# Edge stage of a graph transformer block: VectorE weighs and adds its four slots in 16 small instructions

## The reference, cut to what matters

```python
e = jnp.einsum('ehd,ehd->eh', k[src], q[dst]) / jnp.sqrt(jnp.float32(H * D))
emax = jax.ops.segment_max(e, dst, num_segments=N)
ex = jnp.exp(e - emax[dst])
denom = jax.ops.segment_sum(ex, dst, num_segments=N)
a = ex / denom[dst]
m = v[src] * a[..., None]
ft2 = jax.ops.segment_sum(m, dst, num_segments=N).reshape(N, F)
```

## Time and profile before

| | us |
|---|---|
| median of 3 runs | 2310.03 (2309.44 to 2310.37) |
| profiled execution | 2306.91 |
| its span, first to last instruction | 2305.0 |
| VectorE busy | 1798.8 (78%) |
| TensorE busy (matmuls) | 1829.8 (79%) |
| ScalarE busy | 1505.6 (65%) |
| GpSimd busy | 1304.2 (57%) |
| edge stage, first gather to last fold | about 105 to 1461 |

### The profile page before, as it was taken

The page is one execution under the profiler, slowest core; times in us unless marked ns, Lnnn a source line. Parts: engine busy times, 40 slices in busy tenths (PEclk is TensorE's granted clock), DMA queues, the critical chain, the costliest instruction groups (busy, mean ns, idle before and its releaser), DMA issues. The chain is left out here.

```text
span 2305.0 us, 43942 instructions
## 1 busy us (share of the span) xinstructions
PE 1829.8 (79%) x12285; PEld 1288.0 (56%) x12285; DVE 1798.8 (78%) x3579; ACT 1505.6 (65%) x5102; POOL 1304.2 (57%) x1281
## 2 busy tenths in 40 slices
PE   7768787788776688887888871387999769999996
PEld 3423333333333566666666650233888669999995
DVE  7389999999998999999999998555899864444442
ACT  2267787777776587787877874587555355555553
POOL 0177777777777777777777777276000014444442
PEclk9878898999988688897978975599999889999998
DMA  8677777777777777777777777475010282222223
GB/s 231 189 229 226 225 229 230 226 222 228 219 225 225 211 226 224 231 226 231 228 230 235 222 234 220 123 201 161 12 32 29 69 294 42 37 36 36 36 37 77
DMA packets 213270, 394.32 MB, mean 171 GB/s; under 512 B 46354, under 2 KB 140637, under 8 KB 213005
## 3 DMA queue, kind: packets, MB, share of 16 engines
q0 software_dynamic: 91392, 278.99, 43.0%
q1 hardware_dynamic: 96848, 90.41, 13.3%
q10 hardware_dynamic: 24829, 22.64, 3.0%
HBM read 346.47 MB, written 48.65 MB: 171 GB/s over the span
## 5 line engine op out<-in xcount | busy, mean ns | idle before, releaser
L802 POOL DMA_INDIRECT ring<-kv_tab,idx x1008 | 1029.3, 1021 | 412.4 <-issue 294.6
L1120 ACT ACTIVATE val<-ring,val 128x64 f32<-128x64 f32 x2016 | 530.1, 337 | 55.6 <-DVE part L901 51.9
L853 DVE TENSOR_TENSOR prod<-ring,tile_bank 128x1024 f32<-128x1024 f32 x252 | 302.1, 1215 | 32.8 <-DMA ring<-kv_tab,idx 32.2
L860 DVE TENSOR_REDUCE score<-prod 128x16 f32<-128x1024 f32 x252 | 299.1, 1211 | 0.0
L2137 POOL DMA_INDIRECT x_sum<-e_yw,to_row x56 | 123.7, 2210 | 219.3 <-DVE e_yw L2163 197.9
L2122 POOL DMA_INDIRECT xr<-rows,from_row x56 | 57.3, 1024 | 286.7 <-issue 286.4
L2212 PE MATMUL e_h<-e_xT,e_now 128*128 128x128 f32 x1792 | 210.9, 277 | 0.8 <-DVE e_now L2153 0.8
L2212 PEld LDWEIGHTS e_h<-e_xT,e_now 128*128 128x128 f32 x1792 | 206.1, 193 | 1.2 <-DVE e_now L2153 1.2
L2227 PE MATMUL e_yps<-e_now,e_hT 128*128 128x256 f32 x896 | 202.5, 379 | 0.0
L890 DVE TENSOR_TENSOR val<-val 128x1040 f32<-128x1040 f32 x126 | 155.9, 1237 | 52.6 <-ACT val L1120 52.4
L2177 ACT ACTIVATE e_now<-e_w_all 128x2048 f32 x56 | 106.9, 1912 | 131.2 <-PE e_yps L2227 131.2
(11 more groups left out here) (423 smaller groups left out, 4719.1 us busy)
## 6 DMA issues: line engine op xcount, KB each, us to landing
loaded<-parts SPq DMA_DIRECT2D x150, 130.0 KB, 2.3
e_w_all<-L_ffn_W SPq DMA_DIRECT2D x16, 1024.0 KB, 12.2
parts<-part ACTq DMA_DIRECT2D x126, 130.0 KB
q_win<-q_tab SPq DMA_DIRECT2D x126, 128.0 KB
ring<-kv_tab,idx POOLq DMA_INDIRECT x1008
kv_tab<-kv_t SPq DMA_DIRECT2D x25, 224.0 KB
xn_buf<-x SPq DMA_DIRECT2D x25, 125.0 KB
x_sum<-x_buf SPq DMA_DIRECT2D x25, 125.0 KB
```

The lines of the kernel that those rows point to most:

```text
L802: pool.indirect_dma_start(out=ring[:, n % RING, e, :], out_offset=None, in_=t.kv_tab, in_offset=bass.IndirectOffsetOnAxis(ap=idx[n % 6][:, ...
L853: dve.tensor_tensor(prod[half][:, :, :], ring[:, n % RING, at, 0:F], bcast(q_ps[n % 2].unsqueeze(1), 128, L // 2, F), ALU.mult).then_inc(q ...
L860: dve.tensor_reduce(score[:, at, :], prod[half][:, :, :].rearrange("p s (h d) -> p s h d", h=HG), AX.X, ALU.add).then_inc(reduced, 1)
L1120: one = act.activation(val[n % 2][:, e, h, 0:DG], ring[:, n % RING, e, F + h * DG:F + (h + 1) * DG], ACT.Copy, scale=val[n % 2][:, e, h, D ...
```

## The change

`weigh` and `fold` go. In their place `weigh_onto` computes, for one slot and head of VectorE's half at a time, value times factor plus ScalarE's weighed value of the slot four further on, 64 elements with the factor read as one number for each partition from column `DG` of `val`. There are 16 such instructions in a tile, eight (slots 0 and 1) in the place of `weigh`, eight (slots 2 and 3) in the place of `fold`. Since their factor column must stay until they are done, `add_factors` first sums the 16 factor pairs into `part_w`, and `keep_factors` copies them back behind the 16. Each run of eight waits for ScalarE's slots that it adds; ScalarE now signals after every slot. The exponentials into `w_ps`, its PSUM region and its semaphore go, and with them the waits of `times_q`, `exps` and `q_of_rows` on them. GpSimd's wait counts the new signals.

```diff
--- before.py
+++ after.py
@@ -717,6 +717,7 @@
         foreign = [s.sb(f"foreign{i}", [128, L]) for i in range(6)]
         prod = [s.sb(f"prod{i}", [128, L // 2, F]) for i in range(2)]
         score = s.sb("score", [128, L, HG])
+        part_w = s.sb("part_w", [128, L // 2, HG])
         own = s.sb("own", [128, L, HG])
         less = [s.sb(f"less{i}", [128, L, HG]) for i in range(2)]
         val = [s.sb(f"val{i}", [128, L, HG, DG + 1]) for i in range(2)]
@@ -754,7 +755,6 @@
         q_ps = [b[:, 0:F] for b in tile_banks]
         where_ps, local_ps = ([tile_banks[(n + 1 - AHEAD) % 2][:, at:at + size] for n in range(2)]
                               for at, size in ((F, 2 * L + 1), (F + 64, 128)))
-        w_ps = [tile_banks[(n + 1) % 2][:, F + 192:F + 192 + L // 2 * HG].rearrange("p (s h) -> p s h", h=HG) for n in range(2)]
         kf_ps = bank_f[0:TP, 0:NPAIR]
         gT_ps = [b[:, 0:NPAIR] for b in (bank_g, bank_o)]
         normT_ps = bank_f2[:, 0:NPAIR]
@@ -772,8 +772,8 @@
 
         blocks_in, q_in, landed, part_out = (x.blocks_in, s.sems("q_win_in", 3), s.gather_sems("landed", 8),
                                              s.sems("part_out", 3))
-        compared, found, idx_ready, spread_ready, find_read, placed, gap_ready, places, w_ready = (
-            s.sem("e_" + n) for n in ("compared", "found", "idx", "spread", "find_read", "placed", "gap", "places", "w_ps"))
+        compared, found, idx_ready, spread_ready, find_read, placed, gap_ready, places, factors_added = (
+            s.sem("e_" + n) for n in ("compared", "found", "idx", "spread", "find_read", "placed", "gap", "places", "factors"))
         q_ready, q_read, reduced, scored, top_ready, less_ready, exp_ready, val_ready, act_val_ready, folded, folding, sum_ready, part_ready, carrier = (
             s.sem("e_" + n) for n in ("q", "q_read", "reduced", "scored", "top", "less", "exp", "val", "act_val", "folded", "folding", "sum", "part", "carrier"))
         level_split, level_in = s.sem("level_split"), s.sem("level_in")
@@ -795,8 +795,8 @@
         def _(pool):
             for n in range(TILES):
                 pool.wait_ge(idx_ready, n + 1)
-                wait(pool, val_ready, n - RING + 1)
-                wait(pool, act_val_ready, n - RING + 1)
+                wait(pool, val_ready, 2 * (n - RING + 1))
+                wait(pool, act_val_ready, 4 * (n - RING + 1))
                 pool.sem_inc(carrier, 1)
                 for e in range(L):
                     pool.indirect_dma_start(out=ring[:, n % RING, e, :], out_offset=None, in_=t.kv_tab,
@@ -848,7 +848,6 @@
                 dve.wait_ge(landed[n % RING * 2 + half], 16 * (L // 2) * (n // RING + 1))
                 dve.wait_ge(q_ready, n + 1)
                 dve.wait_ge(find_read, min(n + AHEAD, TILES))
-                wait(dve, w_ready, n)
                 wait(dve, reduced, 2 * n + half - 1)
                 dve.tensor_tensor(prod[half][:, :, :], ring[:, n % RING, at, 0:F], bcast(q_ps[n % 2].unsqueeze(1), 128, L // 2, F),
                                   ALU.mult).then_inc(q_read, 1)
@@ -877,20 +876,29 @@
                 dve.tensor_tensor(less[n % 2][:, :, :], own[:, :, :], bcast(t.m_all[:, n, :].unsqueeze(1), 128, L, HG),
                                   ALU.subtract).then_inc(less_ready, 1)
 
-            def weigh(n):
-                dve.wait_ge(w_ready, n + 1)
-                dve.tensor_tensor(val[n % 2][:, 0:L // 2, :, 0:DG],
-                                  ring[:, n % RING, 0:L // 2, F:2 * F].rearrange("p s (h d) -> p s h d", h=HG),
-                                  bcast(w_ps[n % 2].unsqueeze(3), 128, L // 2, HG, DG), ALU.mult).then_inc(val_ready, 1)
-
-            def fold(n):
-                v = val[n % 2][:, :, :, :].rearrange("p s h d -> p s (h d)")
-                dve.wait_ge(val_ready, n + 1)
-                dve.wait_ge(act_val_ready, n + 1)
-                dve.tensor_tensor(v[:, 0:4, :], v[:, 0:4, :], v[:, 4:8, :], ALU.add).then_inc(folding, 1)
+            def add_factors(n):
+                v = val[n % 2]
+                dve.wait_ge(exp_ready, n + 1)
+                dve.tensor_tensor(part_w[:, :, :], v[:, 0:4, :, DG], v[:, 4:8, :, DG], ALU.add).then_inc(factors_added, 1)
+
+            def weigh_onto(n, slots):
+                v = val[n % 2]
+                dve.wait_ge(exp_ready, n + 1)
+                dve.wait_ge(act_val_ready, 4 * n + slots.stop)
+                for e in slots:
+                    for h in range(HG):
+                        one = dve.scalar_tensor_tensor(v[:, e, h, 0:DG], ring[:, n % RING, e, F + h * DG:F + (h + 1) * DG], v[:, e, h, DG:DG + 1],
+                                                       v[:, L // 2 + e, h, 0:DG], ALU.mult, ALU.add)
+                one.then_inc(val_ready, 1)
+
+            def keep_factors(n):
+                dve.wait_ge(val_ready, 2 * n + 2)
+                dve.wait_ge(factors_added, n + 1)
+                dve.tensor_copy(val[n % 2][:, 0:4, :, DG], part_w[:, :, :]).then_inc(folding, 1)
 
             def fold_on(n):
                 v = val[n % 2][:, :, :, :].rearrange("p s h d -> p s (h d)")
+                dve.wait_ge(val_ready, 2 * n + 2)
                 dve.wait_ge(folding, 2 * n + 1)
                 dve.tensor_tensor(v[:, 0:2, :], v[:, 0:2, :], v[:, 2:4, :], ALU.add).then_inc(folding, 1)
 
@@ -1071,7 +1079,8 @@
                 if now:
                     keep_own(n)
                 if old:
-                    weigh(n - 1)
+                    add_factors(n - 1)
+                    weigh_onto(n - 1, range(0, 2))
                 if now:
                     top(n)
                 mix(n, 2, 1)
@@ -1080,7 +1089,8 @@
                 mix(n, 2, 2)
                 mix(n, 3, 0)
                 if old:
-                    fold(n - 1)
+                    weigh_onto(n - 1, range(2, 4))
+                    keep_factors(n - 1)
                 if n + AHEAD + 1 < TILES:
                     compare(n + AHEAD + 1)
                 if old:
@@ -1107,8 +1117,6 @@
 
             def exps(n):
                 act.wait_ge(less_ready, n + 1)
-                act.wait_ge(q_ready, min(n + 2, TILES))
-                act.activation(w_ps[n % 2], less[n % 2][:, 0:L // 2, :], ACT.Exp, scale=1.0 / float(F) ** 0.5).then_inc(w_ready, 1)
                 wait(act, folded, n - 1)
                 act.activation(val[n % 2][:, :, :, DG], less[n % 2][:, :, :], ACT.Exp, scale=1.0 / float(F) ** 0.5).then_inc(exp_ready, 1)
 
@@ -1119,8 +1127,7 @@
                 for h in range(HG):
                     one = act.activation(val[n % 2][:, e, h, 0:DG], ring[:, n % RING, e, F + h * DG:F + (h + 1) * DG], ACT.Copy,
                                          scale=val[n % 2][:, e, h, DG:DG + 1])
-                if e == L - 1:
-                    one.then_inc(act_val_ready, 1)
+                one.then_inc(act_val_ready, 1)
 
             def keep_part(n):
                 act.wait_ge(folded, n + 1)
@@ -1213,7 +1220,6 @@
                 pe.wait_ge(q_in[n % 3], 16 * (n // 3 + 1))
                 pe.wait_ge(spread_ready, n + 1)
                 wait(pe, q_read, 2 * n - 2)
-                wait(pe, val_ready, n - 2)
                 pe.matmul(q_ps[n % 2], spread[n % 6][:, :], q_win[n % 3][:, :], start=True, stop=True).then_inc(q_ready, 1)
 
             def late(u, kind):
```

## The result

| | before | after |
|---|---|---|
| median, us | 2309.74 (2305.88 to 2310.37) | 2396.32 (2394.77 to 2402.74) |
| ratio | | 1.0372 (1.0355 to 1.0389) |
| profiled execution, us | 2306.91 | 2402.74 |
| span, us | 2305.0 | 2400.9 |

The forecast was 2408, with a range of 2350 to 2470. The profiled execution is the slowest of the four, 6.4 us above their median.

The account below looks back on a forecast made before the run. VectorE and GpSimd were taken to bound the edge stage together. Its four stretches, +50, +3, +44 and +1, sum to +98 us on the profiled 2306.91, giving 2405; the run median lies 3.1 above, 2408, range 2350 to 2470.

Parts of the forecast that it names:

- What bounds the stage: Edge stage: GpSimd at 10.6 us a tile and VectorE at 10.15 and 9.70 are at their limit together.
- The step of the 16: Added VectorE instructions of 64 elements: 0.195 us each start to start, 3.12 us a tile, ends 2.3 and 4.5.
- Sums, copy and the wait: VectorE: factor sum and copy 0.09 us each, wait for the last of the 16 0.085; together 0.27 a tile.
- Collisions: VectorE's small instructions meeting gathers: some 2.5 a tile at 0.04 to 0.07, 0.1 us, ends 0 and 0.3.
- VectorE net: VectorE's added work less the removed weighing and fold: +1.21 us a tile, ends 0.2 and 2.9.
- GpSimd near 10.6, VectorE ahead: Gathers: a hit costs about 0.2 us, two or three a tile; GpSimd stays near 10.6, VectorE at 11.4 sets the pace.
- Slack: VectorE's idle time in the edge stage's four stretches absorbs part of the added work, leaving +50, +3, +44 and +1 us.
- Held gathers: Rival, edge stage: runs of eight hold GpSimd out, which then needs 11.9 us a tile; +167, 2477 us; chance 12%.
- ScalarE: Rival, edge stage: ScalarE sets the pace, slots 4 and 5 late at the first run; +140, 2450 us; chance 11%.
- Half rate: Rival: the 16, with two fp32 SBUF inputs, run at half throughput; 1.07 us a tile more, 2543 us; chance 2%.
- Cheap instructions: Rival: the 16 step by 0.11 us and GpSimd is freed; 2286 us, or slack hides it, 2310; chance 6%.
- 16 places, 11 for it: Trace before: in 11 of 16 places a gather gets in between two adds instead of outlasting the next one too.

Follow-up runs that it names:

- filler_320: The kernel before plus one VectorE sum a tile over 320 copies of a constant, 0.4 us, one input: 2323.18 us, ratio 1.0042.
- the split folds: The kernel before with its first fold in two adds of 520 elements or four of 260: 2301.87 us (0.9953) and 2301.75 us (0.9951).
- filler_1088_b: The kernel before plus one VectorE sum a tile over 1088 copies of a constant, 1.2 us, one input: 2386.40 us, ratio 1.0307.
- imm_factor_b: The changed kernel with an immediate 1.0 for the factor per partition: 2335.67 us, ratio 1.0080; as imm_factor on the slow chip 2806 us, 0.9825.

## Why the prediction was right

- *What bounds the stage.* Two engines, VectorE and GpSimd: shown from both sides, by `filler_320` (0.4 us a tile costs 9.7 us, not 50) and by the split folds (more VectorE work, 0.5% faster). `filler_1088_b` gives 3.1 of the 3.7%.
- *The step of the 16*, taken as 0.195: 0.196. The row that it was taken from, the same operation at 256 elements, was the right neighbour; the lower end, 0.145 without the factor, is 0.136 in `imm_factor_b`.
- *Sums, copy and the wait*, 0.27: the sum takes 0.10 in the mean of the first stretch (0.14 in the lines shown, 502.04 to 502.18), the copy 0.08, the wait 1.69 - 1.57 = 0.12: about 0.3. *Collisions* were small, since all steps within the runs of eight are 0.197 in the mean.
- *VectorE net*, +1.21 a tile: busy time rose by 58.9 us in the first stretch and 60.3 in the third, 1.09 and 1.12 a tile. The sum was 0.1 too high, and the collisions were the term that was not there. (Its ends, 0.2 and 2.9, come to 0.1 and 2.8 from the terms given.)
- *GpSimd near 10.6, VectorE ahead*: GpSimd came to 8 x (0.968 + 0.30) = 10.1, better than forecast. A hit costs 0.03 us, not 0.2, and the mean gather lies below the 1.00 to 1.04 us forecast. It changed nothing, for VectorE at 11.47 was the bound in either case.
- *Slack.* First stretch +50 and measured +50.2; second +3 and +3.9; third +44 and +34.1; fourth +1 and -1.9. The third is the term furthest off: I had 1.21 us of work added and 0.43 us of idle time left a tile; it was 1.12 and 18.9 / 54 = 0.35, together 0.17 less, 9 us, and its period, 602.9 / 54 = 11.16, is below the 11.4 to 11.6 forecast. In the first the +50 is right by luck, by two errors that cancel: 0.12 less work, and 12.5 / 54 = 0.23 idle left where I had 0.10.
- *The rivals.* Held gathers: excluded by 968 ns. ScalarE: 26.8 us of waits, inside the 15 to 30 forecast; against the filler some 10 us of them belong to the change, and the sum had no term for it. Half rate: from 64 to 256 elements the duration with a factor goes from 277 to 480 ns, 1.06 ns an element. Cheap instructions: 0.196 is not 0.12.
- *A right total with one lucky sign.* That gathers get in between was read from 16 places, 11 for it. It holds for this instruction almost always, and for its form with an immediate mostly not (102 of 137). The trace before has no run of such small instructions and could not show that difference. What it could show is that its five held places are all the same pair, L901 followed by L650, where it happened five times in six.

## What to carry to other kernels

Cost a small VectorE instruction by its step, start to start, from a row of the same operation with the same kinds of operands: the factor per partition was 0.06 of 0.196 us here, and 16 of them cost more than the two wide ones that they replaced. When two engines bound a loop together, work added to one costs little up to the slack and nearly all of itself beyond it; two fillers of different length find that point. And where instructions with two inputs in SBUF stretch gathers, and the engine that issues the gathers is a bound, try cutting the long ones in two: it cost VectorE time and still won 0.5%.

## What the runs showed of the hardware

- A gather issued by GpSimd is stretched by VectorE instructions with both inputs in SBUF: 1022 ns in the mean with a fold of 1040 elements, 1009 and 1002 with the fold in two and four, 968 with the 16 that read a factor per partition, 1045 with the same 16 and an immediate. A sum of 1.27 us with one input stretches none (120 gathers, 0.003 us at most).
- SBUF — State Buffer in the Trainium skill, "SBUF: two separate sides", has the pair of interfaces held for one whole instruction. The fold in two agrees (45 of 49 gathers get in between its adds), and so does the changed kernel (0.13 us late at most). The run of 64-element instructions with an immediate does not: it holds a gather over up to eight of them.
- A number read per partition adds 0.06 us to the step and to the duration of an instruction on two tensors (0.196 against 0.136 us and 277 against 219 ns at 64 elements).
- That instruction on two fp32 tensors in SBUF takes 219 ns at 64 and 419 ns at 256 elements with an immediate, 1.04 ns an element, and with a factor per partition 277 and 480 ns.
- One chip ran the same kernel at 2857 us instead of 2310; TensorE's granted clock in `imm_factor` there was 0.81, in the same kernel elsewhere 0.87, and the cause is open. A comparison holds only within one chip, and on that one not for a question of a few per cent.
